# A two-layer cross-attention kernel: values and scores on 64-row tiles, the values' halves added in HBM, x issued by ScalarE, front and end reordered

## The reference, cut to what matters

```python
q = (x @ Wq + bq)                       # (b, 1024, 32 heads, 32)
k = ctx @ Wk + bk ; v = ctx @ Wv + bv   # (b, 64, 8 heads, 32)
scores = einsum('bkgld,bksd->bkgls', q, k) * 32 ** -0.5 + mask
out = einsum('bkgls,bksd->bkgld', softmax(scores), v)
x1 = layernorm(out @ Wo + bo + x) * gamma + beta
# layer 1: another cross-attention with 16 heads of 64 on x1, with residual
```

## Time and profile before

| | us |
|---|---|
| median of 3 runs | 1742.0 (1741.31 to 1742.42) |
| the profiled execution | 1743.04 |
| its span in the profile | 1741.2 |
| TensorE busy | 1710.5 (98%) |

### The profile page before, as it was taken

One profiled execution on the slowest core, in us unless ns is written; L12 is line 12 of the kernel. 1 busy time (PEld: TensorE's weight loads), 2 busy tenths in 40 slices (PEclk: granted clock), 3 DMA queues, 4 the chain that ended last, 5 costly groups with the idle time before them and its releaser, 6 DMA issues.

```text
span 1741.2 us, 22386 instructions
## 1 busy us (share of the span) xinstructions
PE 1710.5 (98%) x8449; PEld 1428.8 (82%) x8449; DVE 1169.3 (67%) x1109; ACT 581.8 (33%) x670; POOL 1068.2 (61%) x589
## 2 busy tenths in 40 slices
PE   6999999999999999999999999999999999999998
PEld 6888888888888778888878877888888888888887
DVE  6899898888988666565646578446644664466443
ACT  4344454444444433333334223122312231223110
POOL 2677877878788866665756453446734673467331
PEclk9999999999999999999999999999999999999999
DMA  8443343332236577777766856555545654565332
GB/s 238 103 111 83 80 108 104 84 85 73 75 99 177 175 231 239 224 231 229 235 213 211 263 184 194 169 169 180 171 158 169 181 169 156 171 185 166 133 108 98
DMA packets 276335, 280.11 MB, mean 161 GB/s; under 512 B 62330, under 2 KB 228356, under 8 KB 275972
## 3 DMA queue, kind: packets, MB, share of 16 engines
q1 hardware_dynamic: 275776, 276.97, 52.1%
q10 hardware_dynamic: 452, 1.71, 0.3%
HBM read 175.81 MB, written 102.76 MB: 160 GB/s over the span
## 4 chain that ended last, share of the span: by engine, by line
PE 84%; POOL 5%; DVE 4%; issue 3%; DMA 2%; ACT 1%; SPq 1%; POOLq 0%; DVEq 0%
PE ps L53 27%; PE ps L54 27%; PE ps L55 27%; PE ps L723 1%; PE ps L731 1%; POOL xb L1426 1%; POOL wqsl L1458 1%; POOL y L1440 1%; DMA wv0r<-in_L_xattn_Wv_dram 1%; DMA ocr<-o_scratch 1%; POOL oc1l L1421 0%; DVE wTl L1186 0%; SPq L475 0%; DMA xd<-x_scratch 0%; DVE y L1209 0%
## 5 line engine op out<-in xcount | busy, mean ns | idle before, releaser
L1477 POOL TENSOR_TENSOR x2Tl<-x2r,x2Th 128x1024 fp32r<-128x1024 f32 x31 | 74.5, 2404 | 275.2 <-ACT x2Th L985 275.2
L1254 DVE STREAM_TRANSPOSE x2r<-xd 128x1024 f32<-128x1024 f32 x32 | 68.8, 2150 | 200.8 <-PE ps L55 200.6
L1411 POOL TENSOR_TENSOR pr<-pr,small 128x1024 f32<-128x1024 f32 x64 | 122.0, 1906 | 100.7 <-DVE small L1142 100.7
L985 ACT CAST x2Th<-x2r 128x1024 fp32r<-128x1024 f32 x32 | 33.7, 1053 | 366.6 <-DVE x2r L1254 366.6
L1406 POOL TENSOR_TENSOR pr<-pr,small 128x1024 f32<-128x1024 f32 x64 | 122.0, 1906 | 11.3 <-DVE small L1120 9.2
L1426 POOL TENSOR_TENSOR xb<-xb,bo 128x1024 f32<-128x1024 f32 x32 | 77.9, 2434 | 72.2 <-DMA xb<-in_x_dram 72.2
L1440 POOL TENSOR_TENSOR y<-y,bet 128x1024 f32<-128x1024 f32 x31 | 74.3, 2397 | 54.5 <-DVE y L1172 54.5
L1116 DVE TENSOR_REDUCE small<-pr 128x16 f32<-128x1024 f32 x64 | 78.1, 1220 | 42.5 <-ACT pr L866 42.5
L53 PE MATMUL ps<-xT0h,wq0l 128*128 128x512 f32 x256 | 100.8, 394 | 3.7 <-DVE wq0l L1071 3.7
L53 PE MATMUL ps<-wo0h,oc1l 128*128 128x512 f32 x256 | 102.2, 399 | 1.9 <-POOL oc1l L1421 1.4
L1172 DVE TENSOR_TENSOR y<-y,gam 128x1024 f32<-128x1024 f32 x32 | 54.1, 1691 | 74.3 <-ACT y L906 74.3
(11 more groups left out here) (382 smaller groups left out, 5450.1 us busy)
## 6 DMA issues: line engine op xcount, KB each, us to landing
xr<-in_x_dram SPq DMA_DIRECT2D x128, 128.0 KB, 2.8
o_scratch<-ot SPq DMA_DIRECT2D x256, 64.0 KB, 1.8
ocr<-o_scratch SPq DMA_DIRECT2D x16, 1024.0 KB, 7.9
xb<-in_x_dram SPq DMA_DIRECT2D x32, 512.0 KB, 7.0
a_scratch<-ost SPq DMA_DIRECT2D x64, 256.0 KB, 3.4
b_scratch<-ost SPq DMA_DIRECT2D x64, 256.0 KB, 5.9
xd<-x_scratch SPq DMA_DIRECT2D x128, 128.0 KB, 2.9
raw<-b_scratch SPq DMA_DIRECT2D x64, 256.0 KB, 5.7
```

The costliest lines, as they stand in the source:

```text
L1254: nc.vector.transpose(x2r[:].rearrange("p k (t j) -> p t k j", t=TPB), xd[:].rearrange("p t (i k) -> p t k i", k=KT)).then_inc(x2_turned, 1)
L1411: nc.gpsimd.tensor_tensor(heads(v), heads(v), mx.unsqueeze(2).to_broadcast([P, TPB * GRP, KEYS]), ALU.subtract)\
L1477: nc.gpsimd.tensor_tensor(x2T[1][:], x2r[:], f32(x2T[0][:]), ALU.subtract).then_inc(x2_lo, 1)
```

## The change

- **Scores**: K is no longer used as 128 rows. Two matmuls of 64 rows each (partitions 0 to 63 and 64 to 127) take two heads each: 24 matmuls of 128 columns instead of 12 of 256. `qs` has one buffer instead of two.
- **Values**: `vb` holds for each 64-row half the high and the low part of V side by side, so the stationary operand is 64 x 128 and all four products h and l are made: 8 matmuls of 64 rows and 512 columns instead of 6 of 128 rows. The output is twice as large (128 x 1024, both banks of V): one half of the result in each of two scratch tensors, `o` and `ol`. They are added in HBM by one DMA of 256 KB for each unit, issued by GpSimd with `accum_op`, seven slots after the unit. The copy into `ot` (L877) is 128 x 1024, the four stores are 128 KB each, and chunks of `o` wait for the sum.
- **Order on TensorE**: the query's k = 0 to 5 first, then values, scores, and k = 6 and 7.
- **x tiles** in the units are issued by ScalarE after the query's high part, no longer by SyncE.
- **Front and end**: the first x tiles are split earlier and among three engines, the low part of K goes to GpSimd, and near the end two low parts change their place.

```diff
@@ TensorE
-                    after(pe, o_ev, v - 1)
-                    for c in range(2):
-                        last = three(nc, V[v % 2], [vb[v % 2][:, c, x] for x in (0, 1)], [pT[v % 2][x][:, c]... for x in (0, 1)],
-                                     c == 0, c == 1)
+                    after(pe, o_ev, v)
+                    for n, (c, x) in enumerate(((0, 1), (0, 0), (1, 1), (1, 0))):
+                        for h in range(2):
+                            rows = slice(64 * h, 64 * (h + 1))
+                            last = nc.tensor.matmul(V[h], vb[v % 2][rows, c].rearrange("p x a d -> p (x a d)"),
+                                                    pT[v % 2][x][rows, c].rearrange("p j n -> p (j n)"), start=n == 0, stop=n == 3)
...
                 if u < UNITS:
-                    query(range(0, 4))
+                    query(range(0, 6))
                 if 4 <= u < UNITS + 2:
                     values_of(u - 4)
-                if u < UNITS:
-                    query(range(4, 6))
...
-                        last = three(nc, S[v % 2][:, 256 * m:256 * (m + 1)], [qs[v % 2][x][:, m] for x in (0, 1)],
-                                     [kb[v % 2][:, :, x] for x in (0, 1)], True, True)
+                        for n, (x, y) in enumerate(((1, 0), (0, 1), (0, 0))):
+                            for r in range(2):
+                                rows = slice(64 * r, 64 * (r + 1))
+                                last = nc.tensor.matmul(S[v % 2].rearrange("p (j m s) -> p j m s", j=GRP, m=TPB)[:, 2 * r:2 * r + 2, m], qs[x][rows, m],
+                                                        kb[v % 2][rows, 2 * r:2 * r + 2, y], start=n == 0, stop=n == 2)
@@ SyncE
-                if u < UNITS and (u == 1 or u and u % 2 == 0) and (n := 6 + u // 2) < NTILE:
-                    sp.wait_ge(x_turned, n - 3)
-                    load_x(sp, n)
...
-                    for a in range(4):
-                        sp.dma_start(d["o"]..., ot[v % 2][32 * a:32 * (a + 1)]...).then_inc(o_st[v % 2], 16)
+                    for i, name in enumerate(("o", "ol")):
+                        for a in range(2):
+                            rows = slice(64 * i + 32 * a, 64 * i + 32 * (a + 1))
+                            sp.dma_start(d[name]..., ot[v % 2][rows]...).then_inc(o_st[v % 2], 16)
@@ ScalarE
+                if u < UNITS and (u == 1 or u and u % 2 == 0) and (n := 6 + u // 2) < NTILE:
+                    act.wait_ge(x_turned, n - 3)
+                    load_x(act, n)
@@ GpSimd, between the scaling (L1406) and the subtraction (L1411)
+                if KT - 1 <= u and (n := u - KT + 1) < UNITS:
+                    pool.wait_ge(o_st[n % 2], 64 * (n // 2 + 1))
+                    after(pool, o_sum, 16 * n)
+                    nc.gpsimd.dma_start(*(d[name][n // KT, n % KT] for name in ("o", "ol")),
+                                        accum_op=ALU.add, max_dma_last_dim=4096).then_inc(o_sum, 16)
@@ VectorE, front
-            for n in range(4):
-                turn_x(n)
+            turn_x(0)
+            split_x(0)
+            turn_x(1)
+            turn_x(2)
...
+            turn_x(3)
+            for n in (2, 3):
                 split_x(n)
             split_wq(0)
```

More of the change, by code:

```diff
@@ L115, in program @@
               for i in range(2)]
-        ot = [at(f"ot{i}", 202 + 2 * i, [P, BLK]) for i in range(2)]
+        ot = [at(f"ot{i}", o, [P, 2, BLK]) for i, o in enumerate((202, 156))]
         mask = [at(f"mask{i}", 192 + i, [P, TPB, KEYS]) for i in range(2)]
@@ L177, in program @@
         V = [ps[:, 3072 + HALF * i:][:, :HALF] for i in range(2)]
+        VV = ps[:, 3072:4096]
         C2 = ps[:, 0:2048]
@@ L185, in program @@
          vfull, v_hi, v_lo, kv_st, vv_st, wq_hi, wq_lo, x_turned, x_hi, x_lo, q_done, q_hi, q_lo, zeroed, mask_ld, scores,
[L186 removed]
+         s_read, maxed, centered, exped, summed, recips, probs, p_turned, p_hi, p_lo, pv, o_ev, o_sum) = (sem(n) for n in (
              "ctx_ld kv_ld0 kv_ld1 b_ld bv_ld b_turned b_done ones ctx_t ctx_hi ctx_lo kv_hi kv_lo k_done v_done kfull k_hi k_lo vfull v_hi "
              "v_lo kv_st vv_st wq_hi wq_lo x_turned x_hi x_lo q_done q_hi q_lo zeroed mask_ld scores s_read maxed centered "
[L189 removed]
+             "exped summed recips probs p_turned p_hi p_lo pv o_ev o_sum").split())
         w_ld, x_ld, k_ld, v_ld, o_st = sems("w_ld", 4), sems("x_ld", 4), sems("k_ld", 2), sems("v_ld", 2), sems("o_st", 2)
@@ L332, in load_chunk @@
                 t, a = divmod(c, BLK // CHUNK)
-                for i in range(2):
-                    sp.wait_ge(o_st[i], 64 * 4 * (t + 1))
+                sp.wait_ge(o_sum, 16 * KT * (t + 1))
                 after(sp, o_done, 4 * (c - 1))
@@ L876, in slot @@
                     after(act, o_st[v % 2], 64 * (v // 2))
-                    nc.scalar.copy(ot[v % 2][:].rearrange("p (j i m) -> p j i m", j=GRP, m=TPB),
-                                   V[v % 2].rearrange("p (j m i) -> p j i m", j=GRP, m=TPB)).then_inc(o_ev, 1)
+                    nc.scalar.copy(ot[v % 2][:].rearrange("p h (j i m) -> p (h j) i m", j=GRP, m=TPB),
+                                   VV.rearrange("p (j m i) -> p j i m", j=2 * GRP, m=TPB)).then_inc(o_ev, 1)
                 if u < UNITS:
                     act.wait_ge(q_done, u + 1)
-                    after(act, scores, u - 1)
-                    nc.scalar.activation(qs[u % 2][0][:], Q[u % 2].rearrange("p (n m) -> p m n", m=TPB), ACT.Identity,
+                    after(act, scores, u)
+                    nc.scalar.activation(qs[0][:], Q[u % 2].rearrange("p (n m) -> p m n", m=TPB), ACT.Identity,
                                          bias=bq[:, u % KT:u % KT + 1]).then_inc(q_hi, 1)
@@ L1150, in slot @@
                     dve.wait_ge(q_hi, u + 1)
-                    nc.vector.scalar_tensor_tensor(out=qs[u % 2][1][:], in0=Q[u % 2].rearrange("p (n m) -> p m n", m=TPB), scalar=bq[:, u % KT:u % KT + 1],
-                                                   in1=f32(qs[u % 2][0][:]), op0=ALU.add, op1=ALU.subtract).then_inc(q_lo, 1)
+                    nc.vector.scalar_tensor_tensor(out=qs[1][:], in0=Q[u % 2].rearrange("p (n m) -> p m n", m=TPB), scalar=bq[:, u % KT:u % KT + 1],
+                                                   in1=f32(qs[0][:]), op0=ALU.add, op1=ALU.subtract).then_inc(q_lo, 1)
                 for g in wq_late(u):
@@ L1184, in split_wt @@
                 def split_wt(f, i):
+                    if f == 0 and i == 0:
+                        dve.wait_ge(o_st[1], 64 * UNITS // 2)
                     dve.wait_ge(wT_hi, 2 * f + i + 1)
@@ L1201, in out_slot @@
                         diagonal(f, 1)
+                if h == 2:
+                    for i in range(2):
+                        part_ = slice(4 * i, 4 * (i + 1))
+                        dve.wait_ge(oc_hi, 4 + i + 1)
+                        nc.vector.tensor_tensor(oT[1][1][:, part_], oc[1][:, part_], f32(oT[1][0][:, part_]),
+                                                ALU.subtract).then_inc(oc_lo, 1)
                 if half == 0 and n:
@@ L1374, in gpsimd @@
                 nc.gpsimd.tensor_tensor(wv[1][:, half(i)], wvr[:, half(i)], f32(wv[0][:, half(i)]), ALU.subtract).then_inc(kv_lo, 1)
+            for h in range(2):
+                pool.wait_ge(k_hi, h + 1)
+                nc.gpsimd.tensor_tensor(kst[h][:, :, 1, :].rearrange("p b (r i) -> p b r i", r=2),
+                                        kf[:, h].rearrange("p (r b i) -> p b r i", r=2, b=BATCH),
+                                        f32(kst[h][:, :, 0, :]).rearrange("p b (r i) -> p b r i", r=2), ALU.subtract)\
+                    .then_inc(k_lo, 1)
+            pool.wait_ge(x_hi, 2)
+            nc.gpsimd.tensor_tensor(xT[0][1][:, :, P:2 * P], xTr[0][:, :, P:2 * P], f32(xT[0][0][:, :, P:2 * P]), ALU.subtract).then_inc(x_lo, 1)
             def norm_coefficients(step):
@@ L1449, in out_slot @@
                     residual(n + 1)
-                if h == 2:
-                    for i in range(2):
-                        chunk_lo(1, i)
                 if half == 0 and n:
```

41 lines of the change are left out of this document (17 added, 24 removed).

## The result

The changed kernel takes 1760.8 us (median of 4 runs, 1759.1 to 1764.8) where the kernel before takes 1742.2 on the same chip: a ratio of 1.0113 (95% interval 1.0099 to 1.0126), by the medians 18.6 us slower. The forecast was +10. The profiled execution took 1759.1, its span is 1757.3, 16.1 more than the span before.

What follows compares the result with a forecast made beforehand. The softmax engines, waiting for each other, were taken to bound the units at 8.23 us. Units 2 to 55 at +17, the last eight at -5 and the front at -2 gave +10: 1752 us, range 1728 to 1782.

Steps and rivals of the forecast that it cites:

- With TensorE at any speed, the softmax engines need 8.23 us for a unit.: Unit loop: the other engines wait for each other, needing only 0.026 us less than TensorE, whatever TensorE saves.
- d - 0.3: Unit loop: GpSimd's DMA issue of d, taken as 1.0 us, less 0.3 cover, lengthens two units by 0.7 us.
- 128 columns give about 0.06, if it stays in proportion: TensorE's scores: 12 pairs of 128 columns take 0.72 to 1.42 us, taken as 0.8; the unit becomes 7.4.
- In the last eight units ... 8 x 0.66 = -5.: Last eight units, without x tiles: a unit takes 7.6 us against 8.26, so 5 us less in all.
- as TensorE is then ahead: Unit loop: the new query and values order and the single buffer for qs and V cost nothing.
- The two low parts moved near the end: 0, give or take 3; nothing there has a fixed queue behind it longer than that.: Near the end: moving two low parts changes the time by 0, give or take 3 us.
- That is 2 x 1.15 = -2 us: Front: two of four x splits and K's low part move before the first weights' split, 2 us less.
- ScalarE's and SyncE's parts at nothing: Units: ScalarE's x issues cost 0.12 us beside GpSimd's larger 0.7; SyncE's doubled stores and the traffic fit; nothing added.
- The additions do not queue up in the units: Rival 4: each addition waits for the one before, GpSimd with it; at 10 us each +155, 1895 us; chance 0.10.
- the first rival: GpSimd's issue is short (d under 0.5) or covered: -10 us, 1732 us; chance 0.20.
- the third: GpSimd's issue costs clearly more than 1.17 us: at 1.8, two units +1.5, 1777 us; chance 0.13.

Runs made afterwards that it cites:

- e4: The kernel before with four of six value matmuls in each unit (low part of V left out): 1736.0 us, 0.9973.
- e11: Changed kernel with the addition issued after the subtraction of the maxima, the first Wo load early, and ScalarE's exponential never behind a cast: 1740.6 us, 0.9991.
- e1: Changed kernel with GpSimd's adding DMA issued after the subtraction of the maximum instead of before it: 1753.5 us, 1.0069.
- e2: Changed kernel without the adding DMA; the second half isn't added to the output, the stores stay: 1742.0 us, 1.0003.
- e5: Changed kernel with the addition issued after the subtraction and the first Wo load at the head of SyncE's slot 56: 1748.1 us, 1.0039.
- e6: Changed kernel with the adding DMA replaced by SyncE's plain HBM-to-HBM copy of 256 KB in every unit: 1746.1 us, 1.0025.
- e9: The kernel before with ScalarE casting one unit's weights of every two behind the next even unit's exponential: 1740.3 us, 0.9991.
- e13: The kernel before with only the change's reordered front and end: 1740.2 us, 0.9988.
- e18: The kernel before with the reordered front and end and ScalarE's later cast together: 1738.5 us, 0.9989.
- e7: Changed kernel with each unit's addition issued as two DMAs of 128 KB instead of one of 256: 1804.6 us, 1.0363.
- e12: Changed kernel with the x tiles issued by SyncE again: 1758.9 us, 1.0105.
- e15: Changed kernel with a third buffer for the last unit's copy of V alone: 1761.6 us, 1.0121.
- e17: e14 with the last two units' additions issued at the end of GpSimd's output slot instead of the head: 1736.7 us, 0.9975.
- e14: e11 with the last unit's copy of V in a third buffer and GpSimd's normTl ahead of the addition: 1741.9 us, 1.0009.
- e16: e14 with the scores back on full 128-row tiles, only the values on 64-row tiles: 1747.6 us, 1.0047.

## Why the prediction was right or wrong

The direction and the range were right (1728 to 1782), and so was the mechanism of the unit loop. The size was not: 18.6 us against 10. The steps that failed are two terms of the sum. The last eight units were put at -5 us, by a TensorE unit of 7.6 and a V buffer that costs nothing, and measured +5.0; the end behind them was put at 0, give or take 3, and measured +5.9. Together they were 16 us too cheap. The loop was put 7 us too dear, which hides almost half of that; so that the sum came within 9 us is in part luck.

- **"With TensorE at any speed, the softmax engines need 8.23 us for a unit."** Right (e4). What they need is an order, not their work: with ScalarE's swap it is at most 8.03 to 8.08 (e11). That second half was visible in the earlier trace rows as the exponential behind the cast.
- **The issue, "d - 0.3" for two units.** Right in kind, and mis-sized: d = 1.0 became 0.79 to 0.80, the cover 0.3 became 0.4, so 0.37 instead of 0.7, and +9.6 instead of +17. e1 shows 5.9 of it by moving the issue. The rest is 1 to 5 us and hardly clear of noise: traces without an issue in that place have 457.1 to 458.8 (e1, e2, e5, e6), and those with the old matmuls 453.5 to 456.0 (the kernel before, e4, e9, e13, e18). That the first addition of two 128 KB costs the same as one of 256 (e7) shows that d is a price per issue.
- **"128 columns give about 0.06, if it stays in proportion", the scores at 0.8.** The step that failed on TensorE. The other bound, 0.118, was the near one: it measured 0.107, or 1.29 us. The unit fell by 0.19 and not by 0.85, and TensorE idled 11.4 us in the window of 444 us instead of 1.1 in each unit. In the unit loop this cost nothing, as the prediction said, but it leaves the last eight units at 8.07, 0.47 over the 7.6 that was forecast.
- **"In the last eight units ... 8 x 0.66 = -5."** It was +5.0. Beside the 0.47 a unit, the sum took no account of the first load of Wo: ScalarE's copy stands behind it, and the single V buffer, costed at nothing "as TensorE is then ahead", has no second bank to go on with. e5 against e1 puts the stall and what follows from it at 5.4 us. What follows is the slow clock in the trace of the changed kernel and in e1's, and VectorE held by GpSimd in those of e12 and e15; which of the two the other executions had is not known. It was in the profile: ScalarE waited 4.85 us for the same load before.
- **"The two low parts moved near the end: 0, give or take 3; nothing there has a fixed queue behind it longer than that."** This failed as well, +5.9, and not through what was moved: e13 and e18, which move it alone, are 2.0 and 0.8 shorter than before. The seam pays for the addition, which the prediction costed at nothing outside the unit loop: without it (e2) the seam is 56.3, doubled stores and all. With it, GpSimd waits for the addition before, its two-input operations come later and meet VectorE's `wTl`, and TensorE waits 6.67 us where it waited 1.54. A third buffer for `ot` takes 2.4 of the 5.9 away (e15); e17 against e14 puts the wait and the meeting behind it at 5.2 us in the kernel of e14. What the addition's traffic costs there no run shows, since e6's seam is long for a reason of its own.
- **"That is 2 x 1.15 = -2 us" for the front.** -0.7 to unit 0, and not clear of noise: traces with the new front have 43.0 to 44.7, those with the old one 43.8 to 45.0. The split of the first weights takes 3.37 us beside GpSimd's split of x, 1.24 in the earlier trace rows; timeline of both:

```profile
27.80 3.37 DVE L1078 TENSOR_TENSOR wq0l<-wq0r,wq0h 128x1024 fp32r<-128x1024 f32 x1
...
26.74 3.35 POOL L1394 TENSOR_TENSOR xT0l<-xT0r,xT0h 128x1024 fp32r<-128x1024 f32 x1
```

- **ScalarE's and SyncE's parts at nothing.** Right for the x issues (e12). Wo is another matter: before, its load was issued 2.8 us ahead of unit 56's addition of mask and scores (504.88 and 507.7) and took 5.0 to land; now it is issued 1.1 us ahead (514.39 and 515.5) and takes 7.4.
- **Rivals.** The additions do not queue up in the units: they land in 4.6 us in the median, and only at the seam, where they take up to 8.2, does one wait for the one before. The issue, 0.79, lies between the first rival (under 0.5) and the third (over 1.17). The sum with the measured terms is -0.7 + 9.6 + 5.0 + 5.9 = 19.8, against 18.6.

## What to carry to other kernels

An engine that the page shows at 98% may still have nothing to give: compare what its neighbours need with it removed, and look for the order that makes their pace, since work taken from it counts only once both are lowered. Before matmuls are split into narrower pairs, price a pair by the shortest one in the trace and count the switches: neighbouring parts share them. A doubled buffer and a DMA that waits at the head of an engine's slot are paid where the pipeline drains, so walk through the last units and the first of the next stage by name, and ask of each buffer what lies over it later. When a run leaves something out and puts something else in its place, look whether the same wait has come back or only the same time.

## What the runs showed of the hardware

- A VectorE operation with two inputs in SBUF does not get in between GpSimd's: it took 8.76 us beside three of them back to back (1.23 alone), 9.09 in e16, 6.34 in the changed kernel, 4.26 beside two, and 2.14 when it met one. The Trainium skill ("SBUF — State Buffer", SBUF: two separate sides) calls the shared port an exclusive lock that is held for one instruction. The trace shows more: the loser stood for three.
- GpSimd's issue of a DMA that adds is 0.79 us for 256 KB and 1.59 for two of 128 KB. The next instruction's row begins 0.55 us into it, but ends 0.8 later than it would have. The addition lands in 4.6 us in the median (3.7 to 8.7).
- Pairs of 64 rows by 128 columns start 0.107 to 0.11 us apart, hardly closer than full matmuls of 256 columns (0.12); changing between full and 64-row tiles costs 0.1 us on each side, and the first pair of 512 columns 0.1 more.
- After 2.83 us of idle time TensorE's granted clock was 0.50 and then 0.67 in the next two windows of 5 us, and query matmuls stood 0.43 us apart instead of 0.23. Pairs of 64 rows by 128 columns stood 0.21 apart instead of 0.107. After 4.28 us of idle time the clock was 0.50 as well; after 2.39 it stayed at 1.00.
